# Graph network kernel: transposes split behind each first layer, four value and gate buffers, row copy ahead of the product, the nodes' norm moved into the node stage

## The reference, cut to what matters

```
h = relu(layernorm(x))
m = silu(silu(edge @ W1 + b1) @ W2 + b2) * sigmoid(silu(edge @ G1 + g1) @ G2 + g2)
x = x + h + segment_sum(m, dst)
```

```
h = relu(layernorm(x))
s = h @ Ws + bs;  r = h @ Wr + br
logit = (mish(s[src] + r[dst])) . aw + ab      (four heads of 16)
out = x + segment_softmax_sum(logit, s[src], dst)
```

## Time and profile before

| what | us |
|---|---|
| median of 3 runs | 5686.99 |
| lowest and highest of the 3 | 5683.77, 5687.02 |
| the profiled execution, its device time | 5684.08 |
| the profiled execution, its span in the trace | 5682.3 |
| PE busy in the span | 1073.8 (19%) |
| DVE busy | 4327.4 (76%) |
| ACT busy | 2902.7 (51%) |
| POOL busy | 3683.9 (65%) |

### The profile page before, as it was taken

The page is one execution under the profiler, slowest core; times in us unless marked ns, Lnnn a source line. Parts: engine busy times, 40 slices in busy tenths (PEclk is TensorE's granted clock), DMA queues, the critical chain, the costliest instruction groups (busy, mean ns, idle before and its releaser), DMA issues. The chain is left out here.

```text
span 5682.3 us, 43566 instructions
## 1 busy us (share of the span) xinstructions
PE 1073.8 (19%) x8383; PEld 482.7 (8%) x8383; DVE 4327.4 (76%) x4070; ACT 2902.7 (51%) x3353; POOL 3683.9 (65%) x3749
## 2 busy tenths in 40 slices
PE   6888888823000000000000000000000000000000
PEld 2333333313000000000000000000000000000000
DVE  6888898734477878787878787877877887778772
ACT  6888888810244444444444444444444444444440
POOL 3556200057677777777777777777777777777756
PEclk9999999955555555555555555555555555555555
DMA  7888877721233233323332333233323323332322
GB/s 210 250 253 249 265 232 235 237 68 44 65 85 85 74 85 85 85 74 84 85 85 73 85 85 82 77 85 85 83 76 85 85 76 82 85 85 75 84 61 49
DMA packets 300617, 629.61 MB, mean 111 GB/s; under 512 B 100533, under 2 KB 103927, under 8 KB 300210
## 3 DMA queue, kind: packets, MB, share of 16 engines
q1 hardware_dynamic: 178672, 501.38, 27.3%
q0 software_dynamic: 119792, 127.75, 11.6%
q10 hardware_dynamic: 2128, 0.23, 0.0%
HBM read 392.83 MB, written 236.16 MB: 111 GB/s over the span
## 5 line engine op out<-in xcount | busy, mean ns | idle before, releaser
L895 POOL DMA_INDIRECT se<-s_proj,idx x3168 | 2991.9, 944 | 965.2 <-issue 958.2
L913 ACT ACTIVATE held_ps<-keepf 128x1536 f32 (+1 forms) x135 | 196.3, 1454 | 1456.9 <-DVE z L996 1421.7
L1132 PE MATMUL a_ps<-r_ident,r_state 128*4 128x128 f32 x1 | 0.4, 374 | 4121.5 <-DVE drop L1161 4121.5
L996 DVE TENSOR_TENSOR z<-se,held_ps 128x1536 f32<-128x1536 f32 x135 | 370.0, 2741 | 457.8 <-DMA se<-s_proj,idx 420.5
L960 ACT ACTIVATE arows<-work_ps 128x1632 f32<-128x1632 f32 x135 | 206.8, 1532 | 741.1 <-DVEq L1032 741.1
L1021 DVE TENSOR_TENSOR wse<-se,ex_ps 128x1536 f32<-128x1536 f32 x135 | 374.0, 2770 | 201.0 <-ACT ex_ps L951 201.0
L1029 DVE TENSOR_TENSOR_SCAN work_ps<-work_ps,wse 128x1632 f32<-128x1632 f32 x135 | 481.3, 3565 | 4.7
L423 DVE TENSOR_TENSOR_SCAN sums<-keepb,sums,msg 128x1024 f32<-128x1024 bf16 x201 | 470.8, 2342 | 0.0
L340 ACT ACTIVATE hidden<-h_ps,r_b1g 128x1024 f32<-128x1024 f32 x404 | 459.9, 1139 | 12.7 <-PE h_ps L286 12.6
L297 PE MATMUL v_ps<-hidden,r_w2g 64*64 64x512 f32 x1616 | 439.0, 613 | 129.8 <-ACT gate L350 125.2
L990 DVE TENSOR_TENSOR_SCAN held_ps<-held_ps,rnew 128x1536 f32<-128x1536 f32 x135 | 454.3, 3365 | 4.7
(11 more groups left out here) (193 smaller groups left out, 4201.5 us busy)
## 6 DMA issues: line engine op xcount, KB each, us to landing
states<-arows SPq DMA_DIRECT2D x135, 864.0 KB, 6.9
rs<-sums SPq DMA_DIRECT2D x135, 768.0 KB, 5.2
edges<-in_edge_attr SPq DMA_DIRECT2D x202, 512.0 KB, 4.5
sums<-rows SPq DMA_DIRECT2D x402, 256.0 KB
keepb<-keep SPq DMA_DIRECT2D x404, 128.0 KB, 3.7
se<-s_proj,idx POOLq DMA_INDIRECT x3168, 2.4
r_base<-in_x POOLq DMA_DIRECT2D x1, 3136.0 KB, 12.7
s_proj<-sr SPq DMA_DIRECT2D x14, 224.0 KB, 2.4
```

What stands on the lines that cost most here:

```text
L895: pool.indirect_dma_start(out=se[b][:, k, :], out_offset=None, in_=D["s_proj"], in_offset=bass.IndirectOffsetOnAxis(ap=node[:, k:k + 1], a ...
L996: nc.vector.tensor_tensor(z[b][:, :, :], se[b][:, :, :].rearrange("p k f -> p f k"), rneg, ALU.subtract).then_inc(z_ready, 1)
```

## The change

- `value` and `gate` have four buffers each, so ACT's `outs(c, 0)` waits for the product of step c-4 (semaphore value c-3) and no longer of step c-2.
- `turn_rows` is split: `turn_rows(c - 2, ..., u)` does four transposes into bank u of `tr_ps`, behind the first layer of half u. Its semaphores `turned` and `rows_ready` become pairs, one for each bank.
- On DVE `to_rows(c - 2)` stands ahead of `product(c)`.
- The nodes' own norm, its root and the two table loads leave `edge_mlp`. In `update_nodes` DVE does it first, over 98 columns and in seven pairs of blocks of 14 columns, with the squares on ACT and the centred values in PSUM.
- In `center` the square is taken by ACT too and the centred block lies in PSUM; the sum of the squares moves behind `project`.
- POOL waits at the end of `edge_mlp` for the load of x.

```
-        value = [sb(f"value{b}", [P, BLK]) for b in range(2)]
-        gate = [sb(f"gate{b}", [P, BLK]) for b in range(2)]
+        value = [sb(f"value{m}", [P, BLK]) for m in range(4)]
+        gate = [sb(f"gate{m}", [P, BLK]) for m in range(4)]
...
-            def turn_rows(c, m):
+            def turn_rows(c, m, k):
                 pe.wait_ge(scanned, c + 1)
-                wait(pe, rows_ready, c * 2)
+                wait(pe, rows_ready[k], c)
                 cols = sums[m][:, :].rearrange("p (e j) -> p j e", j=J)
-                for j in range(J):
-                    last = nc.tensor.transpose(tr_ps[:, j // 4, (j % 4) * P:(j % 4 + 1) * P], cols[:, j, :], R["ident"][:, :])
-                last.then_inc(turned, 1)
+                for j in range(4):
+                    last = nc.tensor.transpose(tr_ps[:, k, j * P:(j + 1) * P], cols[:, 4 * k + j, :], R["ident"][:, :])
+                last.then_inc(turned[k], 1)
...
                     layer2(c, u)
                     if not last:
                         layer1(c + 1, (m + 1) % 4, u, round + (m + 1) // 4)
-                if not first:
-                    turn_rows(c - 2, (m + 2) % 4)
+                    if not first:
+                        turn_rows(c - 2, (m + 2) % 4, u)
...
                 if u == 0:
-                    wait(act, msg_ready, c - 1)
+                    wait(act, msg_ready, c - 3)
...
-            with act.Fori(1, LN1 + 8) as i:
-                for j in range(4):
-                    step(i * 4 + (2 + j), (2 + j) % 4, i * 2 + (j - 1) // 2)
-            act.wait_ge(var_ready, 1)
-            nc.scalar.activation(std[:, :], var[:, :], ACT.Sqrt, bias=epst[:, :], scale=1.0 / F).then_inc(std_ready, 1)
-            nc.scalar.activation(late[:, 0:1], epst[:, :], ACT.Silu).then_inc(std_ready, 1)
-            with act.Fori(LN1 + 8, NI - 1) as i:
+            with act.Fori(1, NI - 1) as i:
...
             def step(c, m, round, pair, first=False, second=False):
-                product(c, m % 2)
                 if not first:
                     to_rows(c - 2, m % 2, pair, first=second)
+                product(c, m)
                 scan(c, m, round, first=first and m == 0)
...
-            def node_mean(k, n):
...
-            def node_base(k, n):
...
+            with dve.Fori(NQ + 3, NI - 1) as i:
                 body(i, 0)
...
             def root(k):
+                act.wait_ge(centered, NS // 2 + k + 1)
+                nc.scalar.activation(sq[:, 0:JB, :], xc, ACT.Square).then_inc(squared, 1)
                 act.wait_ge(var_h, k + 1)
...
+            for k in range(NS // 2):
+                act.wait_ge(centered, k + 1)
+                nc.scalar.activation(sq[:, :, :], wide_x, ACT.Square).then_inc(squared, 1)
+            act.wait_ge(var_x, 1)
+            nc.scalar.activation(var[:, :], var[:, :], ACT.Sqrt, bias=epst[:, :], scale=1.0 / F).then_inc(std_x, 1)
...
-                do(nc.vector.tensor_tensor(xc[:, :, :], base, st[:, :].unsqueeze(2).to_broadcast(wide), ALU.subtract))
-                do(nc.vector.tensor_tensor(sq[:, :, :], xc[:, :, :], xc[:, :, :], ALU.mult))
-                nc.vector.tensor_reduce(st[:, :], sq[:, :, :], AX, ALU.add).then_inc(var_h, 1)
+                nc.vector.tensor_tensor(xc, base, st[:, :].unsqueeze(2).to_broadcast(wide), ALU.subtract).then_inc(centered, 1)
+
+            def spread_of(k):
+                dve.wait_ge(squared, NS // 2 + k + 1)
+                nc.vector.tensor_reduce(st[:, :], sq[:, 0:JB, :], AX, ALU.add).then_inc(var_h, 1)
...
+            x = R["base"]
+            do(nc.vector.tensor_reduce(mean[:, :], x[:, :, :], AX, ALU.add))
+            do(nc.vector.tensor_scalar(mean[:, :], mean[:, :], 1.0 / F, None, ALU.mult))
+            for k, cols in enumerate(pairs):
+                nc.vector.tensor_tensor(wide_x, x[:, cols, :], spread(mean[:, cols]), ALU.subtract).then_inc(centered, 1)
+                dve.wait_ge(squared, k + 1)
+                do(nc.vector.tensor_reduce(var[:, cols], sq[:, :, :], AX, ALU.add))
+            dve.sem_inc(var_x, 1)
+            dve.wait_ge(std_x, 1)
+            do(nc.vector.reciprocal(var[:, :], var[:, :]))
+            for cols in pairs:
+                do(nc.vector.tensor_tensor(wide_x, x[:, cols, :], spread(mean[:, cols]), ALU.subtract))
+                do(nc.vector.tensor_tensor(wide_x, wide_x, spread(var[:, cols]), ALU.mult))
+                do(nc.vector.scalar_tensor_tensor(x[:, cols, :], wide_x, 0.0, x[:, cols, :], ALU.max, ALU.add))
...
                 center(k)
                 if k > 0:
                     project(k - 1)
+                spread_of(k)
                 scale(k)
```

More of the change, by code:

```diff
@@ L155, in edge_mlp @@
         scanned = sem("scanned")
-        turned = sem("turned")
-        rows_ready = sem("rows_ready")
+        turned = [sem(f"turned{k}") for k in range(2)]
+        rows_ready = [sem(f"rows_ready{k}") for k in range(2)]
         stored = [sem(f"stored{b}") for b in range(2)]
@@ L178, in edge_mlp @@
         NQ = NC // Q
-        LN1 = NQ + 3
         WEIGHTS = 12
@@ L206, in store @@
             def store(c, b):
-                sp.wait_ge(rows_ready, (c + 1) * 2)
+                for k in range(2):
+                    sp.wait_ge(rows_ready[k], c + 1)
                 for s in range(2):
@@ L331, in _ @@
             for c in range(NBLK - 2, NBLK):
-                turn_rows(c, c % 4)
+                for k in range(2):
+                    turn_rows(c, c % 4, k)
         @block.scalar
@@ L345, in outs @@
                 if u == 0:
-                    wait(act, msg_ready, c - 1)
-                nc.scalar.activation(value[b][:, half], v_ps[:, :], ACT.Silu, bias=b2[:, :]).then_inc(gated, 1)
+                    wait(act, msg_ready, c - 3)
+                nc.scalar.activation(value[m][:, half], v_ps[:, :], ACT.Silu, bias=b2[:, :]).then_inc(gated, 1)
                 act.wait_ge(g_ready, n + 1)
-                nc.scalar.activation(gate[b][:, half], g_ps[:, :], ACT.Tanh, scale=0.5, bias=g2[:, :]).then_inc(gated, 1)
+                nc.scalar.activation(gate[m][:, half], g_ps[:, :], ACT.Tanh, scale=0.5, bias=g2[:, :]).then_inc(gated, 1)
             def to_rows(c, b, pair):
-                act.wait_ge(turned, c + 1)
+                act.wait_ge(turned[1], c + 1)
                 wait(act, stored[b], pair * 32)
                 nc.scalar.activation(rows[b][:, :, J // 2:J, :].rearrange("p s j f -> p j s f"),
-                                     tr_ps[:, 1, :].rearrange("p (j s f) -> p j s f", s=2, f=F), ACT.Copy).then_inc(rows_ready, 1)
+                                     tr_ps[:, 1, :].rearrange("p (j s f) -> p j s f", s=2, f=F), ACT.Copy).then_inc(rows_ready[1], 1)
             def step(c, m, pair, first=False, last=False):
                 hid(c, 1)
-                outs(c, m % 2, 0)
+                outs(c, m, 0)
                 if not first:
@@ L411, in _, with product @@
         def _(dve):
-            def product(c, b):
+            def product(c, m):
                 dve.wait_ge(gated, 4 * (c + 1))
                 wait(dve, scanned, c - 1)
-                nc.vector.scalar_tensor_tensor(msg[b][:, :], gate[b][:, :], 1.0, value[b][:, :], ALU.add, ALU.mult).then_inc(msg_ready, 1)
+                nc.vector.scalar_tensor_tensor(msg[m % 2][:, :], gate[m][:, :], 1.0, value[m][:, :], ALU.add, ALU.mult).then_inc(msg_ready, 1)
             def scan(c, m, round, first=False):
@@ L420, in scan @@
                 dve.wait_ge(keep_in[m], round * 32 + 32)
-                wait(dve, turned, c - 3)
+                for k in range(2):
+                    wait(dve, turned[k], c - 3)
                 carry = 0.0 if first else sums[(m + 3) % 4][:, BLK - 1:BLK]
@@ L592, in _ @@
             dve.wait_ge(state_ready, 1)
-            dve.wait_ge(rows_ready, NBLK * 2)
+            for k in range(2):
+                dve.wait_ge(rows_ready[k], NBLK)
         @block.gpsimd
@@ L635, in update_nodes @@
         agg = sb("agg", [P, NJ, F])
-        xc = sb("h_xc", [P, JB, F])
-        sq = sb("h_sq", [P, JB, F])
+        mean = sb("mean", [P, NJ])
+        var = sb("var", [P, NJ])
+        sq = sb("h_sq", [P, 2 * JB, F])
         st = sb("h_st", [P, JB])
@@ L653, in update_nodes @@
         src_in = sem("src_in")
+        centered = sem("centered")
+        squared = sem("squared")
+        var_x = sem("var_x")
+        std_x = sem("std_x")
         var_h = sem("var_h")
```

63 lines of the change are left out of this document (13 added, 50 removed).

## The result

The changed kernel takes 5669.4 us (median of 9 runs, 5663.5 to 5674.2), the kernel before in the same runs 5687.1 us: a ratio of 0.9967, with a 95% interval of 0.9957 to 0.9978. It is 17.7 us faster, where 41 us were forecast, and 2.4 us above the range of the forecast. The profiled executions differ by 15.5 us (spans of 5666.8 and 5682.3 us).

The account below looks back on a forecast made before the run. The loop gate, second layer, value was taken as the bound, ACT close behind. Gains 33 + 4 + 6 = 43 less 2 gave 41 us: 5643 on the profile's scale, 5646 us as a median, range 5619 to 5667.

Parts of the forecast that it names:

- The transposes: Edge stage: four transposes behind each first layer, second layer 0.32 us earlier, step from 5.52 to 5.20 us.
- The copy ahead and the four buffers: Edge stage: DVE's row copy moves into its wait of over 1 us; costed at nothing, buffers helping only in the search.
- 5.5 us of room for the store: Edge stage: time from ACT's half of the transposed rows done (952.02) to DVE's next copy (957.6), left for the store.
- 24 x 0.25 = 6 us: Search in the edge stage: 24 rounds of four steps fall from 22.1 to 21.9 us, a gain of 6 us.
- The ring: Search: POOL's eight DMAs 14.54 us, landing 5.30, `find_second` 1.30, back to POOL 0.82; 21.96 us, not shrinking with PE.
- the bound of 0: Search: the lower bound of the gain, a round keeping 22.1 us; the other bound was 30 us.
- fourth rival: Search: more fetches meet a scan, 2.49 us not 0.94; 37 us for each one more a round, two give 5720; chance 0.04.
- The norm leaves the edge stage: Edge stage: delayed steps around the norm vanish, mean step 5.57 to 5.21 us; 33 us over 91.5 steps, transposes' gain included.
- The norm in the node stage: Node stage: DVE's 54 us of new work cost 0, bounds -3 to +3 us; subtractions slow gathers a microsecond or two.
- The cover: Node stage: DVE's 92.7 us wait for the first scatters, behind POOL's 98 gathers, hides the norm's 54 us, about 35 spare.
- Square: Node stage: squares on ACT taken at 0 us; if tables must load, two loads of 1.28 us a block, +5 us.
- Rival 5: Node stage: the square on ACT loads tables, 5 us more, 5651 us; chance 0.09.

Follow-up runs that it names:

- e1: The kernel before with the split transposes alone (four behind each first layer): 6248.1 us against 6273.5 of before, ratio 0.9959.
- e2: The kernel before with four value and gate buffers and the row copy ahead of the product, transposes unsplit: 6233.5 us, ratio 0.9938.
- e7: The changed kernel with the load of x in 14 parts, one every fourth step from step 114 on: 5663.0 us, ratio 0.9962.
- e8: The changed kernel with POOL fetching a round's second lists ahead of the round before's third lists, with second buffers and a later third search: 5634.9 us, ratio 0.9913.
- e3: The changed kernel with the nodes' own norm back between the edge steps and the node stage, its square too, as before: 6217.9 us.
- e6: The changed kernel with a block's sum of squares ahead of the projection of the block before, as it was: 5664.5 us, ratio 0.9960.
- e4: The changed kernel with the mean of the nodes' own norm in PSUM, so its 14 subtractions read one SBUF tensor: 6185.3 us.

## Why the prediction was wrong, point by point

- **The transposes.** Right, and to the size: 5.19 us a step for 5.20, ACT idle 0.27 for 0.28, the second layer 0.15 us behind the gate in both halves. e1 and e2 show that it is this part alone. Steps 111 to 201 gave 34.7 us for 33.
- **The copy ahead and the four buffers, cost nothing.** Right away from the search. What I left out is what the split does when DVE is late: the copy now stands in the way of a second layer. I had looked whether the copy fits, not whom a late copy holds up. It is the step that failed behind the load of x: I named no such load, though it lies at the end of the search. My 5.5 us of room for the store left it out, and the wait for the store that I had put among the signs of being wrong is there, 6.2 us. The two steps behind the load take 11.0 and 6.2 us for 5.2 each, 6.8 us more together, where the kernel before has one of 6.4; 4.5 us of it are PE's wait, in which its clock falls, to stay down for 6.9 us. The 101st step, which takes 9.5 us for 5.5 behind the last late list, is the other part of the 7.4 us that steps 101 to 111 lost, where I had them 3 us faster. e1, e2 and e7 show the part of the load.
- **The search.** The step "24 x 0.25 = 6 us" failed in its sign. The ring was named with its parts, and e8 shows that it is the bound. But I took 21.9 us for it, under its mean. POOL's starts of all 24 rounds give 22.2 us before and 22.4 after: the fetches 15.3 and 15.3 us, the landing 4.9 and 5.0, the rest 2.1. A ring that long can give nothing, and the bound of 0 was the right value. It even got longer. 20 rounds of 0.23 us more are 4.6 of the 7.8 us; the rest is, by my estimate, the lead that the first steps had won: step 21 came 5.8 us earlier, POOL's first round only 1.9 us (82.6 for 84.5), and a loop that a ring holds gives such a lead back. In the eleven traces with this ring the search goes with the ring's mean: 440.9 us with 22.1, 443.0 with 22.2, 450.8 with 22.4, 454.4 with 22.6. What made the landing 0.2 us longer is open. It is not the split alone: e1 has it and a ring of 22.2 us; e2 has not, PE never waits for the copy in its search and its clock never falls there, and yet its ring is 22.5 us and its search 449.4. The late lists, the late copies and the three stretches at half clock are how a late round reaches PE now; whether they also lengthen the ring was not tested alone. My fourth rival had a longer ring too, but by another way: the fetches were to meet more scans and take longer, and they took the same 15.3 us.
- **The norm leaves the edge stage.** Right in its sign; at the new pace it is worth 28 us (e3 against the changed kernel), of which my sum had 5, in the difference of 5.57 and 5.52. The sum still fits, since it took the steps without the norm.
- **The norm in the node stage, cost 0, bounds -3 to +3 us.** The cover held: DVE still waits 57.2 us for the first scatters, and the norm's 54 us were 55 (from 1154.8 to 1209.3). Two terms were mis-sized. The gathers lose 9 us: of 14 subtractions of 1.10 us all but the first hold up a gather, which takes 1.46 to 1.85 us for 0.94. I had read the mild cases (1.2 to 1.4 us, beside instructions of 0.62 us) and called it "a microsecond or two". And POOL waits 7.0 us for blocks: the chain of a block, with the root behind the projection, is 10.2 us for POOL's 9.6. I had written that it gets one step longer, and not added it up. POOL's idle time in the scatters rose from 29.5 to 34.7 us, while its own work fell from 101.7 to 98.2 with the centred block in PSUM: 1.7 us net, and e6 regains 5.6.
- **Square.** No load: the stage has one table load of 1.28 us at its start. Rival 5 is out.
- **The forecast of 5646.** 43 us of gain less 2 became 34.7 + 5.8 - 7.8 - 7.4 - 10.7 = 14.6 us. The gain is there in full, and three places that were put at -6, -3 and 0 gave 26 us back (7.8, 7.4 and 10.7).

## What to carry to other kernels

When an instruction is moved ahead of the one that bounds the loop, ask what it waits for and how late that can be, not only whether it fits in the hole: it takes the slack of all that stood behind it. Look at the clock behind each new wait, too: a wait of PE can cost more than its length. When the bound of a loop falls, write down every ring that spans the loop, and compare its mean over all rounds with the new pace; a ring of 22.2 us under a loop of 22.1 has no gain in it, and swapping the order of two fetches was worth more than the whole change. Work that is hidden in time can still cost through a port: count the vector instructions with two SBUF inputs that run beside indirect DMAs.

## What the runs showed of the hardware that was not expected

- A gather's issue on POOL takes 0.94 us. When it starts inside a DVE subtraction of 128x896 (1.10 us) with two SBUF inputs it takes 1.46 to 1.85 us, in all 13 cases longer by what is left of the subtraction less 0.13 or 0.14 us. The gather at 1161.79, which began 0.02 us ahead of its subtraction, took 0.95 us. Beside the same subtraction with one input in PSUM a gather takes 0.94 again (e4).
- PE's granted clock fell from 1.00 to 0.50 at three waits of 2.2 to 2.5 us in the search, for 3.4 us each, and for 6.9 us at the wait of 4.5 us behind the load of x. Not every wait of that length did it: at one of 2.4 us (up to 396.91 us) the clock stayed at 1.00.
- A scan of DVE right behind the product that it reads had to wait for it 0.25 or 0.38 us in about half of the steps away from the search (13.0 us in 42 waits from 658 to 1133 us). It costs nothing here, as DVE has time.
- One and the same kernel took 5685 to 5687 us in three groups of runs and 6273 in another. The step of 5.19 or 5.52 us in the edge stage and the gathers are the same; some 510 of the 587 us are in the stages behind the last scatter, which are full of indirect DMAs to and from memory.
